# Batch block on one Trainium2 core: eight square-layer differences moved from GpSimd to VectorE, with ring refills, LayerNorm statistics and check pieces in another order

## What is computed

```python
xn = layernorm(x)
qkv = xn @ W_qkv.T + b_qkv                # 16 heads of 16
q, k = elu(q) + 1, elu(k) + 1
att = (q @ (k.T @ v)) / clip(q . k.sum(), 1e-6)
att = layernorm(att @ W_proj.T + b_proj) * gamma + beta + xn
h = silu(xn @ w1.T * s1) * (xn @ w2.T * s2)            # 256 -> 1024
h = gelu(h @ h1.T * s_h1)                              # 1024 -> 1024, first square layer
h = gelu(h @ h2.T * s_h2)                              # 1024 -> 1024, second square layer
out = x + att + h @ w3.T * s3
```

## Time and profile before

| | us |
|---|---|
| median of 3 runs | 1591.0 (1588.35 to 1591.22) |
| the profiled execution | 1589.78 |
| its span | 1587.6 |
| its mean granted TensorE clock | 0.977 of full speed |

### The profile page before, as it was taken

The page is one execution under the profiler, slowest core; times in us unless marked ns, Lnnn a source line. Parts: engine busy times, 40 slices in busy tenths (PEclk is TensorE's granted clock), DMA queues, the critical chain, the costliest instruction groups (busy, mean ns, idle before and its releaser), DMA issues.

```text
span 1587.6 us, 33333 instructions
## 1 busy us (share of the span) xinstructions
PE 1494.1 (94%) x11020; PEld 1294.5 (82%) x11020; DVE 1183.8 (75%) x2208; ACT 926.1 (58%) x1727; POOL 366.9 (23%) x464
## 2 busy tenths in 40 slices
PE   9999899898998989989899998999989989899998
PEld 6988779787797877978778787787878878778787
DVE  6757778677786777867778677786777867778677
ACT  4546656565565656655666465665666646666564
POOL 2203223031220412204122041220412204122030
PEclk9999999999999999999999999999999999999999
DMA  8796726547265472654627546174462744617443
GB/s 236 240 323 227 241 74 221 199 137 250 61 225 192 141 252 64 231 177 154 238 65 239 174 153 237 61 244 169 158 235 61 250 160 156 238 59 250 162 161 134
DMA packets 89090, 287.66 MB, mean 181 GB/s; under 512 B 9696, under 2 KB 55392, under 8 KB 65760
## 3 DMA queue, kind: packets, MB, share of 16 engines
q0 software_dynamic: 43296, 231.75, 43.3%
q1 hardware_dynamic: 44928, 54.29, 10.6%
q10 hardware_dynamic: 832, 1.18, 0.2%
HBM read 270.42 MB, written 25.17 MB: 186 GB/s over the span
## 4 chain that ended last, share of the span: by engine, by line
PE 57%; DVE 14%; issue 10%; ACT 9%; DMA 8%; DVEq 1%; ACTq 0%; SPq 0%
PE ps L1033 22%; DMA raw_weights<-weight_blocks 8%; PE ps L1006 7%; PE ps L1004 7%; PE ps L1120 4%; PE ps L1068 3%; PE ps L893 3%; DVE partial_sums L1753 3%; PE ps L894 3%; PE ps L895 3%; ACT values_a L1372 3%; PE ps L956 2%; PE ps L945 2%; DVE values_b L1728 2%; ACT values_out L1372 1%
## 5 line engine op out<-in xcount | busy, mean ns | idle before, releaser
L1033 PE MATMUL ps<-operands_a,hidden_weights 128*128 128x256 f32 x2520 | 358.8, 288 | 0.0
L1033 PEld LDWEIGHTS ps<-operands_a,hidden_weights 128*128 128x128 f32 x2520 | 328.0, 194 | 0.3
L1033 PE MATMUL ps<-lo_a_in_bits,hidden_weights 128*128 128x256 f16 x2520 | 327.2, 275 | 0.0
L1033 PEld LDWEIGHTS ps<-lo_a_in_bits,hidden_weights 128*128 128x128 bf16 x2520 | 242.9, 99 | 32.2 <-DVE lo_a_in_bits L1703 0.2
L783 POOL DMA_DIRECT2D hidden_weights<-weight_blocks x236 | 128.5, 544 | 578.7 <-PE ps L1033 544.5
L1703 DVE SCALAR_TENSOR_TENSOR lo_a_in_bits<-values_a,operands_a 128x512 f16<-128x512 f32 x315 | 214.6, 704 | 51.9 <-ACT operands_a L1344 40.9
L1033 PE MATMUL ps<-operands_b,hidden_weights 128*128 128x256 f32 x840 | 152.0, 306 | 56.8 <-DVE partial_sums L1753 55.9
L1033 PEld LDWEIGHTS ps<-operands_b,hidden_weights 128*128 128x128 f32 x840 | 122.9, 203 | 63.9 <-issue 61.2
L1033 PE MATMUL ps<-lo_b_in_bits,hidden_weights 128*128 128x256 f16 x840 | 133.8, 284 | 24.1 <-DMA hidden_weights<-weight_blocks 24.1
L1006 PE MATMUL ps<-xnT,w_ffn 128*128 128x512 f32 x512 | 150.5, 421 | 0.0
L1710 DVE SCALAR_TENSOR_TENSOR lo_out_in_bits<-values_out,hidden_out 128x512 f16<-128x512 f32 x120 | 78.6, 687 | 78.2 <-ACT hidden_out L1349 78.2
(11 more groups left out here) (165 smaller groups left out, 2783.0 us busy)
## 6 DMA issues: line engine op xcount, KB each, us to landing
hidden_weights<-weight_blocks POOLq DMA_DIRECT2D x180, 1024.0 KB, 5.2
hidden_weights<-weight_blocks POOLq DMA_DIRECT2D x60, 512.0 KB, 5.1
raw_weights<-weight_blocks SPq DMA_DIRECT2D x70, 231.5 KB, 2.7
hidden_weights<-in_w_ffn POOLq DMA_DIRECT2D x16, 512.0 KB, 8.1
weight_blocks<-weight_sums SPq DMA_DIRECT2D x16, 512.0 KB, 3.5
weight_blocks<-in_w_ffn SPq DMA_DIRECT2D x16, 512.0 KB, 10.5
out_dram<-acc SPq DMA_DIRECT2D x31, 256.0 KB, 2.2
x<-in_H SPq DMA_DIRECT2D x15, 512.0 KB, 6.0
```

The lines of the kernel that those rows point to most:

```text
L1033: r = mm(bank[:, m * HT:(m + 1) * HT], wk, xk, start=i in firsts and begins and m == 0 and j == 0, stop=i in lasts and ends and m == 1 and ...
```

## The change

- `t1`, `t2`, `t3` and `t4` of groups G0 and G1 leave GpSimd and are made by VectorE's functions of the same names, four in each group, written between `gated`, `lo`, `normalise` and `swap` of the gate stage. The semaphore of GpSimd's differences goes.
- In GpSimd's queue the refills of a tile follow each other at once; `inverse_root(t, 1, ...)`, which waits for `ln2_stats`, now stands ahead of `refill(t, 1, 2)` and not behind `refill(t, 2, 0)`.
- On VectorE `ln2_stats` moves from between the low parts of B22 and T3 of the second layer to right behind `ln1_stats`. In its old place stands check piece 2. Piece 0 moves ahead of `lo(G1, T3)`, piece 1 takes piece 0's old place, the old places of pieces 1 and 2 are empty. Pieces 3, 4 and 5 stay.
- The low parts of B21 of the second layer are made ahead of those of T4.

The diff, with the removed GpSimd functions cut to one:

```diff
--- before.py
+++ after.py
@@ -147,10 +147,9 @@
       "H0B22", "H0B11", "H1B11", "H1B22", "H0T1", "H1T1", "H0T2", "H1T2", "H0T3", "H1T3", "H0B21", "H1B21", "H0T4", "H1T4",
       "O0C22", "O1C22", "O0C11", "O1C11", "O0C12", "O1C12", "O0C21", "O1C21")
 LO = ("G0B11", "G0T1", "G0T2", "G1B11", "G1T1", "G0T3", "G1T2", "G1T3", "G0B21", "G1B21", "G0B22", "G1B22", "G0T4", "G1T4",
-      "H0B11", "H1B11", "H0T1", "H1T1", "H0T2", "H1T2", "H0B22", "H1B22", "H0T3", "H1T3", "H0T4", "H1T4", "H0B21", "H1B21",
+      "H0B11", "H1B11", "H0T1", "H1T1", "H0T2", "H1T2", "H0B22", "H1B22", "H0T3", "H1T3", "H0B21", "H1B21", "H0T4", "H1T4",
       "O0C22", "O1C22", "O0C11", "O1C11", "O0C12", "O1C12", "O0C21", "O1C21")
-POOL_T = ("G0T1", "G0T2", "G0T4", "G0T3", "G1T1", "G1T2", "G1T3", "G1T4")
-DVE_T = ("H0T1", "H1T1", "H0T2", "H1T2", "H0T3", "H1T3", "H0T4", "H1T4")
+DVE_T = ("G0T1", "G0T2", "G0T3", "G0T4", "G1T1", "G1T2", "G1T3", "G1T4", "H0T1", "H1T1", "H0T2", "H1T2", "H0T3", "H1T3", "H0T4", "H1T4")
 
 
 class Count:
@@ -411,7 +410,6 @@
     add = Named(sem("products_added"), ADDS)
     lo_half = Named(sem("lo_made"), LO)
     dve_t = Named(sem("difference_made_by_dve"), DVE_T)
-    pool_t = Named(sem("difference_made_by_pool"), POOL_T)
     xnT_split = Count(sem("xnT_split"), DC)
     xnT_cut = Count(sem("xnT_lo_cut_to_16_bits"), 1)
     out_read = Count(sem("output_group_read"), 2, 2)
@@ -490,8 +488,7 @@
         return lo_half.after(t, group + block)
 
     def difference_made(t, group, block):
-        name = group + block
-        return dve_t.after(t, name) if name in DVE_T else pool_t.after(t, name)
+        return dve_t.after(t, group + block)
 
     def value_made(t, group, block):
 
@@ -753,25 +750,6 @@
                 inverse_root(t, 0, ln1_var, ln1_root)
                 tt(rstd_and_one[:], rstd[0][:], ones_row[:], ALU.add).then_inc(ln1_root.sem, 1)
 
-            def t1(t, group):
-                pool.wait_ge(*value_made(t, group, "B12"))
-                tt(value(group, "T1"), value(group, "B12"), value(group, "B11"), ALU.subtract).then_inc(pool_t.sem, 1)
-
...
             def refill(t, turn, g):
 
                 pool.wait_ge(*ring_part_free(t, turn, g))
@@ -828,19 +806,8 @@
 
                 def body(t, more):
                     filling = first == 0
-                    t1(t, "G0")
-                    t2(t, "G0")
-                    t4(t, "G0")
-                    t3(t, "G0")
-                    pool.wait_ge(*lo_made(t, "G1", "B11"))
-                    t1(t, "G1")
-                    t2(t, "G1")
                     if filling:
                         refill(t, 0, 0)
-                    pool.wait_ge(*lo_made(t, "G0", "T3"))
-                    t3(t, "G1")
-                    t4(t, "G1")
-                    if filling:
                         refill(t, 0, 1)
                         refill(t, 0, 2)
                         refill(t, 0, 3)
@@ -848,12 +815,11 @@
                         refill(t, 1, 1)
                     if more:
                         ln1(t + 1)
+                    inverse_root(t, 1, ln2_var, ln2_root)
                     if filling:
                         refill(t, 1, 2)
                         refill(t, 1, 3)
                         refill(t, 2, 0)
-                    inverse_root(t, 1, ln2_var, ln2_root)
-                    if filling:
                         refill(t, 2, 1)
                         refill(t, 2, 2)
                         refill(t, 2, 3)
@@ -1736,10 +1702,13 @@
 
                 if group == "H1":
                     dve.wait_ge(*prod.after(t, "1P4"))
+                if group[0] == "G":
+                    dve.wait_ge(*value_made(t, group, "B22"))
                 dve.wait_ge(*difference_made(t, group, "T1"))
                 difference(t, group, "T2", "B22", "T1")
 
             def t3(t, group):
+                dve.wait_ge(*difference_made(t, group, "T1"))
                 difference(t, group, "T3", "B22", "B12")
 
             def t4(t, group):
@@ -2042,22 +2011,32 @@
                     cut_kv(t, 0)
                     gated(t, 1)
                     cut_kv(t, 1)
+                    t1(t, "G0")
                     lo(t, "G0", "B11", first > 0)
+                    gated(t, 5)
                     lo(t, "G0", "T1", first > 0)
-                    gated(t, 5)
+                    t2(t, "G0")
                     normalise(t, 0)
                     gated(t, 2)
+                    t3(t, "G0")
                     lo(t, "G0", "T2", first > 0)
                     gated(t, 6)
+                    t4(t, "G0")
                     swap(t, 0)
                     gated(t, 3)
+                    t1(t, "G1")
                     lo(t, "G1", "B11", first > 0)
                     gated(t, 7)
+                    lo(t, "G1", "T1", first > 0)
+                    t2(t, "G1")
                     normalise(t, 1)
-                    lo(t, "G1", "T1", first > 0)
                     lo(t, "G0", "T3", first > 0)
                     lo(t, "G1", "T2", first > 0)
                     swap(t, 1)
+                    t3(t, "G1")
+                    t4(t, "G1")
+                    if checking and more:
+                        check_piece(t - 1, 0)
                     lo(t, "G1", "T3", first > 0)
                     lo(t, "G0", "B21", first > 0)
                     lo(t, "G1", "B21", first > 0)
@@ -2075,10 +2054,11 @@
                     lo(t, "G1", "T4", first > 0)
                     if more:
                         ln1_stats(t + 1)
+                    ln2_stats(t)
                     lo(t, "H0", "B11", first > 0)
                     lo(t, "H1", "B11", first > 0)
                     if checking and more:
-                        check_piece(t - 1, 0)
+                        check_piece(t - 1, 1)
                     add_c12(t, 0)
                     add_c12(t, 1)
                     t1(t, "H0")
@@ -2096,24 +2076,20 @@
                     t3(t, "H1")
                     lo(t, "H0", "B22", first > 0)
                     lo(t, "H1", "B22", first > 0)
-                    ln2_stats(t)
+                    if checking and more:
+                        check_piece(t - 1, 2)
                     lo(t, "H0", "T3", first > 0)
                     lo(t, "H1", "T3", first > 0)
                     add_u(t, 2)
                     add_u(t, 3)
                     t4(t, "H0")
                     t4(t, "H1")
-                    if checking and more:
-                        check_piece(t - 1, 1)
+                    lo(t, "H0", "B21", first > 0)
+                    lo(t, "H1", "B21", first > 0)
                     lo(t, "H0", "T4", first > 0)
                     lo(t, "H1", "T4", first > 0)
-                    lo(t, "H0", "B21", first > 0)
-                    lo(t, "H1", "B21", first > 0)
                     if more:
                         transposed_lo(t + 1, 0)
-                    if checking and more:
-                        check_piece(t - 1, 2)
-                    if more:
                         transposed_lo(t + 1, 1)
                     add_w(t, 2)
                     add_w(t, 3)
```

12 lines of the change are left out of this document (removed).

## The result

The changed kernel takes **1492.41 us** (median of four runs, 1491.84 to 1493.73), the kernel before 1590.95 us (1588.35 to 1591.22): a ratio of 0.9385, interval 0.9369 to 0.9402. Forecast were 1513 us, in a range of 1484 to 1549. The profiled execution took 1492.58 us, 97.2 less than that of before (1589.8). So direction, range and the stops that go were right, and the gain was a quarter larger than forecast (97 against 77 us).

A forecast was written before the change was run, and what follows sets the result against it. TensorE's three second-layer stops, 14 times over, were taken as the bound. Per body 7.9 - 1.0 - 0.2 - 1.2 = 5.5 us, times 14 is 77 us: 1589.8 - 77 = 1512.8, say 1513 us, range 1484 to 1549.

The forecast's parts named there:

- What bounds the kernel: Second layer: TensorE stops 0.49 us before product 7, 1.71 before product 2, 3.53 before product 3, in each of 14 bodies.
- What goes: Per body: 3.9 us waiting on VectorE's sums, 1.7 on the weight ring, 2.3 of low clock, together 7.9 us.
- the 2.3 taken from the mean clock: Half clock behind the stop before product 3: mean clock 0.977 over a 98.65 us body, 2.3 us a body to go.
- (a): Gate stage: differences delay gated(t, 3), so product 1 waits for G1's B11 high part; new 1.0 us stop, bounds 0.3 to 2.5.
- (b): GpSimd queue: refill(t, 1, 2), now behind inverse_root(t, 1), lands about when product 5 wants it; 0.2 us, bounds 0 and 1.5.
- (c): Tail: less lead for output operands delays V's bias addition, last K and V steps wait; 1.2 us, bounds 0 and 3.5.
- 2.3 us lost lead: Tail: output operands start 7.9 us before product 4 ends, formerly 10.2; some 1.2 us of the loss come back.
- The cause of the long stop: Before product 3: VectorE idles 4.57 us for check piece 2, whose load could start only after piece 1, some 7 us before.
- R2: Tail takes over: ScalarE and VectorE chain stops TensorE 3.5 us, clock falls again (1.5 us); 1566 us, chance 0.08.
- R3: Check piece 2, ahead of add_u, still stops VectorE 2 us if its load takes 12 us; 1541 us, chance 0.07.
- R4: Slower: VectorE becomes the bound, eight subtractions cost 4.8 us a body, stop at product 1 lowers the clock; 1600 us, chance 0.04.
- The rule on shared ports: Gate stage: two-input VectorE and SBUF-reading GpSimd instructions block each other; VectorE regains 0.4 us a body, forecast sum unchanged.

The follow-up runs named there:

- The experiment on the tail: Changed kernel with T1 of G0 ahead of cut_kv(t, 1), T3 behind gated(t, 3), plus V's bias additions and Q's steps ahead of LayerNorm steps and first output half: 1471.58 us.
- the second experiment: Kernel before with the eight differences moved from GpSimd to VectorE and nothing else moved: 1603.5 us, ratio 1.0089.

## Why the prediction was right, and where it was off

**What bounds the kernel: right.** Three stops of TensorE in the second layer, 14 times over, and they went.

**What goes: right in kind, low by some 0.7 us a body.** Forecast 7.9 us. By the starts in tile 8, product 7 gained 0.74 us, product 2 1.87, product 3 3.70, against idle times of 0.49, 1.71 and 3.53: each stop had cost 0.16 to 0.25 us more than its recorded idle time, 0.6 in all, which the sum left out. Product 3, high and low parts, took 3.65 us (eight groups of four matmuls, 827.65 to 831.30) where it took 6.43 before (880.75 to 887.18), 2.8 more; tile 8 is one of the dear bodies. Over all of them the 2.3 taken from the mean clock was a little high: in the 5.00 us behind the 14 long stops TensorE made 370 matmuls, and at full clock it makes 44 in such a stretch, 616 in all; the 246 that are missing are worth 28 us, 2.0 a body. So what went is 7.9 + 0.6 - 0.3 = 8.2 us a body by its terms, and 8.4 to 8.7 by the difference, the 6.9 us measured and the new stops of 1.5 to 1.8 below.

**(a) The stop in product 1: right.** Forecast 1.0 us, naming the high part of G1's B11; it is there and costs 0.87 by the starts, of which 0.59 is recorded as idle time. `gated(t, 3)` starts 0.7 us ahead of the high part (778.17 and 778.91).

**(b) `refill(t, 1, 2)` behind the root: too high.** Forecast 0.2 us, measured none: no wait for the ring stands in these bodies, and the run with the root moved back takes the same time.

**(c) The tail: right in kind, too high.** Forecast 1.2 us; the last K and V steps do wait for the bias addition, but for 0.16 and 0.36 us in tile 8. By the starts it costs 0.9 there: from the last output matmuls to the next tile's first gate matmul 4.29 us (847.73 to 852.02), and 3.35 before (903.45 to 906.80). More of the 2.3 us lost lead came back than the 1.2 reckoned. The experiment on the tail got 8.1 us back, 0.6 a body over the run.

For tile 8 alone every term is measured: 0.74 + 1.87 + 3.70 + 2.8 = 9.1 us went, 0.9 and 0.9 came, 7.3 in sum, and the body became 7.1 us shorter (98.85 to 91.73). Over the run the sum is 6.4 to 6.9 us a body, not 5.5. The gain was low, the costs were high, and all the errors pointed one way; that is the 20 us.

**The cause of the long stop: half right.** The prediction put it to piece 2's late load, and took its 7 us as what a piece costs at worst. That 7 us was itself made by the late root: the same piece at the same place lands in 2.6 us when the two held refills leave earlier. The forecast did not need this, since the change moved both; that the wrong cause did it no harm is luck. Whoever had forecast the statistics alone with the same working, as the expectation of that run did, was out by 48 us.

**The rivals.** R2: the tail did take a stop, of 0.5 us and not 3.5, and no half clock followed. R3: no piece stopped VectorE in any tile; landing took longer in the median than before (4.3 against 2.7 us on the two pages), but the loads of pieces 2 and 3 have 10.1 and 11.0 us of lead in tile 8. The closest is one whose lead the prediction did not reckon: piece 4, loaded at 828.87 and used at 837.30, has 8.4 us for a landing of 6.7. R4: the subtractions cost 0.87 us a body, not 8.6. The Trainium skill's rule of occupancy (Perfetto Trace Analysis, "Identifying the Most-Contended Engine") would, between VectorE and GpSimd, have kept the work off the one at 75%, and the sign of the second experiment agrees with it. But VectorE is at 83% now and delays TensorE in two places of 0.9 us each, both a matter of order.

**The rule on shared ports.** The Trainium skill, SBUF — State Buffer, "Who interferes with whom", foresaw that VectorE's low parts would run undisturbed once GpSimd stopped subtracting. They do. In the gate stage and behind it, tile 8 after:

```profile
L1669 DVE SCALAR_TENSOR_TENSOR lo_a_in_bits<-values_a,operands_a x10: 664/684/693, 770.4 to 788.9; 128x512 f16<-128x512 f32 x10
```

The 1117 ns of the earlier trace rows is gone. Over the run the mean is 683 ns after and 704 before, and the experiments part in the same way: 706 where GpSimd subtracts (the moves alone), 684 where it doesn't (the differences alone). The trace agrees with the rule, and as forecast it is worth nothing that shows in time here: 5 us of VectorE over the whole run.

## What to carry to other kernels

Before moving work off a waiting engine, follow the wait back through every queue: here one set of statistics held a root, which held two transfers, which delayed one on another queue, and TensorE paid for it twice and then again in its clock. When two stops lie close together, try each suspected cause alone; if each repair brings most of the gain, they share a cause, and the cheapest repair (here two steps on two engines) is the one to take. And when work joins a busy engine, look for the one consumer that is due right behind it: two steps placed anew took back 12.7 us, with the engine as busy as ever.
